# A fused cross-attention, attention and expert kernel: order of work at the two ends of its two-tile part, and fewer zero products at two norms

## What is computed

```python
# x: (1, 64, 256), context: (1, 6272, 256)
h = layernorm(x)
q = rmsnorm_per_head(h @ Wq.T); kv = context @ [Wk; Wv].T
k = rmsnorm_per_head(k_raw)                       # over the 8 numbers of each head
attn = softmax(q k^T * 8 ** -0.5)                 # 32 heads, 64 x 6272
x = x + attn @ v
x = x + self_attention(layernorm(x))              # 16 heads of 128, weights as codes times scales
x = x + experts(layernorm(x))                     # shared expert and 8 experts, top 2
```

## Time and profile before

| | us |
|---|---|
| median of 3 runs | 207.59 (207.58 to 207.79) |
| the profiled execution's own time | 208.22 |
| its span, first to last instruction | 206.4 |
| TensorE busy | 193.7 (94%) |
| ScalarE busy | 148.6 (72%) |
| VectorE busy | 124.7 (60%) |
| GpSimd busy | 109.5 (53%) |

### The profile page before, as it was taken

One profiled execution on the slowest core, in us unless ns is written; L12 is line 12 of the kernel. 1 busy time (PEld: TensorE's weight loads), 2 busy tenths in 40 slices (PEclk: granted clock), 3 DMA queues, 4 the chain that ended last, 5 costly groups with the idle time before them and its releaser, 6 DMA issues.

```text
span 206.4 us, 7072 instructions
## 1 busy us (share of the span) xinstructions
PE 193.7 (94%) x2625; PEld 133.0 (64%) x2625; DVE 124.7 (60%) x326; ACT 148.6 (72%) x286; POOL 109.5 (53%) x131
## 2 busy tenths in 40 slices
PE   7796987999999999999999999999997989999995
PEld 3364564777777777777777777777764553559554
DVE  1588868566767766677676667767533052463680
ACT  2474885889888888998888889888869912342240
POOL 6445759488666848857684885768475001000100
PEclk9999999999999999999999999999999999999999
DMA  6679999999999999999899899999985599100000
GB/s 195 174 195 205 169 234 213 211 175 245 248 208 237 215 223 233 173 259 210 216 210 240 215 210 254 207 259 203 254 198 110 174 405 430 64 0 3 3 0 13
DMA packets 66549, 39.70 MB, mean 192 GB/s; under 512 B 53858, under 2 KB 60642, under 8 KB 66402
## 3 DMA queue, kind: packets, MB, share of 16 engines
q1 hardware_dynamic: 66098, 38.98, 85.8%
q10 hardware_dynamic: 432, 0.46, 0.7%
HBM read 26.52 MB, written 0.07 MB: 129 GB/s over the span
## 4 chain that ended last, share of the span: by engine, by line
PE 71%; ACT 7%; issue 6%; DMA 5%; DVE 5%; POOL 3%; SPq 1%; DVEq 0%; ACTq 0%; POOLq 0%
PE ps L885 17%; PE ps L907 10%; PE ps L862 10%; PE ps L910 8%; PE ps L913 8%; PE ps L960 5%; ACT room L464 4%; DMA kT<-k 3%; PE ps L1054 3%; DMA wkv_f<-xwkv 2%; PE ps L1013 2%; PE ps L1072 2%; PE ps L819 1%; POOL w_all L385 1%; PE ps L999 1%
## 5 line engine op out<-in xcount | busy, mean ns | idle before, releaser
L464 ACT ACTIVATE room<-ps 128x1024 f32<-128x1024 f32 x98 | 95.3, 1023 | 1.8 <-PE ps L862 1.6
L403 POOL TENSOR_TENSOR ctx_lo<-ctx_f,ctx_hi 128x256 fp32r<-128x256 f32 x49 | 36.0, 734 | 43.6 <-DVE ctx_hi L640 40.6
L885 PE MATMUL ps<-room,v_sb 128*27 128x192 f32 (+1 forms) x1176 | 48.4, 310 | 0.2 <-ACT room L464 0.2
L907 PE MATMUL ps<-wkv_hi,ctx_hi 128*128 128x512 f32 x98 | 41.9, 428 | 2.4 <-DVE k L671 2.1
L910 PE MATMUL ps<-wkv_lo,ctx_hi 128*128 128x512 f32 x98 | 39.0, 398 | 1.2 <-DVE wkv_lo L592 1.2
L885 PEld LDWEIGHTS ps<-room,v_sb 128*27 128x27 f32 (+1 forms) x1176 | 32.8, 103 | 11.0 <-ACT room L464 0.6
L385 POOL TENSOR_TENSOR w_all<-w_all,s_ring 128x1024 f32<-128x1024 f32 x16 | 38.2, 2390 | 0.0
L647 DVE TENSOR_REDUCE k_ss<-k_sq 128x32 f32<-128x256 f32 x49 | 20.3, 415 | 29.2 <-ACT k_sq L471 29.2
L390 POOL TENSOR_TENSOR k<-k_n,k 128x256 f16<-128x256 f32 x49 | 32.9, 673 | 6.7 <-DVE k L671 6.7
L862 PE MATMUL ps<-q_blk,kT 48*128 48x128 f16 x784 | 31.5, 218 | 3.9 <-ACT room L464 2.1
L862 PEld LDWEIGHTS ps<-q_blk,kT 48*128 48x128 f16 x784 | 22.0, 94 | 19.1 <-issue 11.0
(11 more groups left out here) (117 smaller groups left out, 134.2 us busy)
## 6 DMA issues: line engine op xcount, KB each, us to landing
w_all<-codes SPq DMA_DIRECT2D x16, 512.0 KB, 4.2
ctx_f<-ctx_t SPq DMA_DIRECT2D x48, 128.0 KB, 3.6
up_sb<-up_w SPq DMA_DIRECT2D x5, 704.0 KB, 7.4
s_ring<-scales SPq DMA_DIRECT2D x12, 256.0 KB
s_ring<-wo_scales SPq DMA_DIRECT2D x4, 512.0 KB
dn_sb<-down_w SPq DMA_DIRECT2D x1, 1792.0 KB, 14.0
kT<-k SPq DMA_TRANSPOSE x49, 4.3
wkv_f<-xwkv SPq DMA_DIRECT2D x1, 256.0 KB, 3.9
```

Source lines behind the costliest of these rows:

```text
L403: nc.gpsimd.tensor_tensor(ctx_lo[:, split.slot(2)], ctx_f[:, split.slot(4)], ctx_hi[:, split.slot(2)].bitcast(F32), ALU.subtract).then_inc ...
L464: nc.scalar.activation(probs[:, t.probs_slot(), half], ps_scores[half].rearrange("p b n -> p (b n)"), ACT.Exp).then_inc(exp_done, 1)
L885: last = nc.tensor.matmul(ps_o[bank][CT * j:CT * j + heads * VW, at:at + heads * N], v_sb[:, t.slot(8), slot:slot + heads].rearrange("p h ...
L907: nc.tensor.matmul(dst, ctx_hi[:, a, c], wkv_hi[:, c], start=(c == 0), stop=False)
```

## The change

- `LOOP0` goes from 4 to 6: two more tiles ahead of the loop are written out, two fewer behind it. The number of trips stays 4.
- `singly` is true behind t = 44 in place of t = 42.
- TensorE, start: at t = 3 scores 3, values 2, projection 8; at t = 4 scores 4, projection 9, values 3.
- TensorE, end: at t = 43 scores 43, projection 48; at t = 44 scores 44, values 42 and 43.
- ScalarE, start: square 7, (3,0), root 7, (3,1), square 8, root 8; then (4,0), (4,1), square 9, root 9.
- ScalarE, end: (43,0), (43,1), square 48; then (44,0), root 48, (44,1).
- `keep_busy` 7 to 5 ahead of the norm of x1, 4 to 2 ahead of that of x2.

VectorE, GpSimd and SyncE keep their order.

```diff
-LOOP0 = 4
+LOOP0 = 6
@@ singly
-    return t.i is None and (t.c < PAIR0 or t.c > PAIR1)
+    return t.i is None and (t.c < PAIR0 or t.c > PAIR1 + 2)
@@ ScalarE, step
-                if not t.odd():
+                if t.i is None and t.c == PAIR0:
+                    keys_squared(r.ahead(-1))
+                    exps(t, 0)
+                    keys_rms(r.ahead(-1))
+                    exps(t, 1)
                     keys_squared(r)
-                if t.i is None and t.c == PAIR0:
+                    keys_rms(r)
+                elif t.i is None and t.c == PAIR1 + 2:
                     exps(t, 0)
-                    keys_squared(r.ahead(-1))
+                    keys_rms(r.ahead(-1))
                     exps(t, 1)
-                    keys_rms(r.ahead(-1))
                 else:
+                    squared_first = not t.odd() and not (t.i is None and t.c == PAIR0 + 1)
+                    if squared_first:
+                        keys_squared(r)
                     exps(t, 0)
                     exps(t, 1)
-                if t.odd():
-                    keys_squared(r)
-                keys_rms(r)
+                    if not squared_first:
+                        keys_squared(r)
+                    if t.i is not None or t.c <= PAIR1:
+                        keys_rms(r)
@@ TensorE, step
+            def all_values(pv):
+
+                for group in range(len(GROUPS)):
+                    if pv.exists():
+                        values(pv, group)
+
                 if singly(t):
-                    for group in range(len(GROUPS)):
-                        if pv.exists():
-                            values(pv, group)
+                    all_values(pv)
...
+                elif t.i is None and t.c == PAIR0:
+                    all_values(pv)
+                    project_context(kv)
+                elif t.i is None and t.c == PAIR0 + 1:
+                    project_context(kv)
+                    all_values(pv)
                 elif t.odd():
                     project_context(kv)
-                    project_context(kv.ahead(1))
+                    if kv.ahead(1).exists():
+                        project_context(kv.ahead(1))
                 else:
-                    for k in (pv.ahead(-1), pv):
-                        for group in range(len(GROUPS)):
-                            values(k, group)
+                    all_values(pv.ahead(-1))
+                    all_values(pv)
@@ TensorE, behind the tiles
-            keep_busy(7)
+            keep_busy(5)
...
-            keep_busy(4)
+            keep_busy(2)
```

## The result

| | before | after |
|---|---|---|
| median of 4 runs, us | 207.69 (207.58 to 208.18) | 204.40 (204.14 to 204.57) |
| the profiled execution's own time, us | 208.22 | 204.50 |
| its span, us | 206.4 | 202.5 |

The ratio is 0.9834 (95% interval 0.9817 to 0.9852). The change is worth 3.29 us between the medians; 3.14 had been forecast. In the changed kernel lines stand 5 to 8 further down: scores are L870, values L893, a projection L915, L918 and L921, zero products L827, the turning L818 and L821, keys times scales L679.

What follows compares the result with a forecast made beforehand. TensorE was taken to bound the two-tile loop and ScalarE its end, with a serial part behind. Start 1.02, end 1.72 and norms 0.40 sum to 3.14 us, taking the median from 207.59 to 204.45, range 203.9 to 205.6.

Steps and rivals of the forecast that it cites:

- The bound and the method: Whole kernel: TensorE bounds the loop, ScalarE the end, then a serial part; only the two ends and serial part change.
- Start, TensorE and ScalarE: Start of two-tile part: waits of 0.55 and 1.51 us go, projection 11 waits about 0.9 us, TensorE gains 1.15.
- Transposed keys, the cover of this: SyncE's queue at the start: keys of tile 4 keep 0.7 us of cover, about 1.3 us more slip stays hidden.
- the prediction's signs: Expected in the trace: projection 9 without wait, projection 11 near 37.9 after about 0.9 us for scaled keys, loop shifted 1.0.
- the list of what would be wrong: Keys 4 waiting over 1.3 us, transposed-key waits over 0.3 us from 130 to 145, or gaps between exponentials of tiles 45-48.
- the term of 1.02: Start's gain kept in the loop's steady state: 1.02 us, bounds 0.6 and 1.3.
- the leads of 0.88 and 1.15: Start of two-tile part: ScalarE's exponentials 5 come 0.88 us earlier, TensorE's projection 11 gains 1.15 us.
- rival A: Start gives little that lasts because transfers fix when keys land; 0.6 to 1.02 us lost, 205.05 to 205.47; chance 0.15.
- The loop: Late keys in the loop shift along with TensorE's pace: taken as 0, bounds 1.02 us loss and 0.3 gain.
- End: End of two-tile part: ScalarE's 1.79 us idle before square 48 goes, 1.72 us gained, bounds 1.0 and 1.8.
- Rival B: End gives half: late transposed keys of tiles 44-48 or scores 45 idle ScalarE 0.9 us; 205.35 us; chance 0.09.
- Norms: Two norms behind the tiles: fewer zero products gain 0.2 and 0.18 us, together 0.40, bounds 0.2 and 0.45.

Runs made afterwards that it cites:

- scales_late: Changed kernel with the 256 KB load of scales 2 issued behind keys 5 instead of ahead: 204.88 us, ratio 0.984 to the kernel before.
- keys6_held: Changed kernel with the transposition of keys 6 held on SyncE until keys 5 have landed: 206.88 us, ratio 0.9918 to the kernel before.
- loop_only: Kernel before with LOOP0 = 6 alone, same order of work on every engine: 207.92 us against 207.94, ratio 0.9987.
- norms_only: Kernel before with 5 and 2 zero products in place of 7 and 4 at the norms, nothing else: ratio 0.9943.
- end_tensor: Kernel before with TensorE's new order at the end alone, ScalarE's order there kept: 207.69 us, ratio 0.9984.
- end_only: Kernel before with the end's new order on TensorE and ScalarE alone, LOOP0 left at 4: ratio 0.9909.
- loop0_5: Changed kernel with LOOP0 = 5, the loop begun one tile earlier: 204.04 us, ratio 0.9824 to the kernel before.
- again: The changed kernel run once more, unaltered: 205.06 us, ratio 0.9875 to the kernel before.
- start_only: Kernel before with the start's new order on TensorE and ScalarE and LOOP0 = 6, end and norms as they were: ratio 0.9942.
- values2_behind: Changed kernel with scales 2 loaded behind keys 5 and projection 8 ahead of values 2 again: 204.03 us, ratio 0.9814 to the kernel before.

## Why the prediction held, step by step

**The bound and the method** held. The two ends and the two norms were the places to gain, and the pace of the loop did not change.

**Start, TensorE and ScalarE: right as far as it went.** Taken from 0.90 us earlier, as scores 3 were, the forecast times are values 2 28.3 (was 28.29), projection 8 29.3 (29.30), scores 4 30.9 (30.90), projection 9 31.45 (31.45), values 3 33.05 (33.04). Projection 9 without a wait, projection 11 waiting 0.50 us 9.07 behind scores 3 in `scales_late`: the order of events was the one worked out from ScalarE's steps.

**The step that failed is "Transposed keys, the cover of this".** It looked at the keys of tile 4 alone. Those were as said: landed 4.1 us after their issue, ahead of scores 4. The next tile was not looked at. Scores 5 stood at 36.96 in the kernel before, keys 5 were issued there at 29.94 and landed 4.5 us later, at about 34.5. The forecast moved scores 5 to 34.95 and so left 0.5 us of cover, where one transfer in the earlier trace rows needed 6.97: the risk could be read before. The issue did not shift (28.95, with the 0.90 of the head 29.85), the transfer took 6.6 us with the scales ahead of it, and the 1.51 us wait followed. So two of the prediction's signs were off: projection 11 stood at 37.67 + 0.90 = 38.57 in place of 37.9, without the wait for scaled keys, and the list of what would be wrong watches keys 4 alone.

**What that wait cost.** In the forecast a new wait of about 0.9 us for scaled keys stands ahead of projection 11. A wait for keys 5 takes its place up to that size, and only what exceeds it is lost. Over six executions the wait for keys 5 and the gain from scores 3 to scores 8 were 1.51/0.44, 1.39/0.58, 0.99/0.96, 0.88/1.07, 0.78/1.18 and none/1.18: gain = 1.18 less what the wait exceeds 0.8, to within 0.03 us. (`keys6_held` is left out, as its edit adds a wait of its own.) So the term of 1.02 was right in size when the keys come in time, 0.16 too low even, and this execution got 0.44. (The prediction does not work out how 1.02 follows from the leads of 0.88 and 1.15; it is their mean.) That is rival A's effect, at the low end of the price that it named (0.58 lost of 0.6 to 1.02), and its mechanism for one transfer: keys 5 were issued where they had been, while the step that wants them came 2 us earlier.

**The loop** was taken at 0 with up to 0.3 of gain if the delay of the late keys vanishes. It did vanish in this execution, and 0.31 us came of it, but that is chance and no part of the change. In the kernel before, scores 40 and 41 wait 0.20 and 0.07 us for late keys:

```profile
142.43 0.62 PE L862 MATMUL ps<-q_blk,kT 48*128 48x128 f16 x16 [0.20 <-DMA kT<-k]
```

From scores 8 to scores 43 ten of the fourteen traces take 104.08 us, in the old order (`loop_only`, `norms_only`, `end_tensor`) as in the new. The kernel before took 104.47, the changed kernel 104.16, `end_only`, which waits for such keys again, 104.56, and `loop0_5` 104.27.

**End: right**, 1.78 against 1.72, by the steps described: square 48 at 151.57 straight behind exponentials 43, root behind (44,0), nine exponentials in 8.61. This execution is a good one: over the nine traces with the new end the gain is 1.5 to 1.8 us. What the forecast did not say is how much each engine's order is worth; ScalarE's is two thirds of it. Rival B showed itself in small: in seven of the nine, scores 45 wait 0.11 to 0.32 us for their keys.

**Norms: right**, 0.43 against 0.40.

**The sum** hit by luck, in part. The start's missing 0.58 was mostly made up by 0.31 in the loop, which is chance, and by 0.06 at the end and 0.03 at the norms. That leaves 2.96 us where 3.14 were forecast; the 0.90 of the head is no part of the change. The medians lie 3.29 apart. A start that gives up to 1.18, as in `again`, would account for the difference, but the unprofiled executions have no trace that shows it.

## What to carry to other kernels

When a step is moved earlier on the bounding engine, check the cover of every transfer that feeds the steps behind it, not only of the first: here tile 4's keys had cover and tile 5's had not. When two waits stand in a row on one engine, removing the first can be free or worthless depending on what releases the second; price the last one. Filler products ahead of a wait could be cut here to about the length of that wait, but not to nothing.

## What the runs showed of the hardware beyond that

**The granted clock fell in seven of the fourteen traces, each time behind an idle of TensorE of 1 to 2 us.** It goes with a part of the spread of timed runs. Of the 33 executions of the kernel before in the first set, the 17 with a full mean clock took 207.10 to 208.28 us, the 13 with a mean of 0.991 or 0.992 took 207.59 to 209.81. It isn't all of it: the six executions of `start_only` with a full clock still lie from 206.11 to 208.11. In the profile of `start_only` the old end leaves TensorE idle for 1.06 us up to 154.11; then, in the table by stretches:

```profile
154.00:156.00 2.00, 1.80 (x40) 1.12 (x40) 1.02 (x2) 1.97 (x5) 0.35 (x1) 1.00 0.70 131
156.00:158.00 2.00, 1.60 (x24) 1.02 (x28) 0.00 (x0) 2.00 (x3) 2.00 (x2) 0.62 0.23 45
158.00:160.00 2.00, 2.00 (x40) 1.17 (x34) 0.00 (x0) 0.78 (x2) 0.64 (x1) 0.52 0.47 86
```

The clock is 0.62 and 0.52 there, the lower level of 1.2 GHz for most of both stretches, and values that take 1.07 us elsewhere took 1.93. The same idle of 1.06 us in the kernel before went without a fall, so a gap makes a fall possible, not certain. In `keys6_held` it fell behind the 1.95 us wait, in `again` from 18 us on, behind a wait of 1.31 us for the queries that ended at 16.53, and in the same place in `loop_only`, `scales_late` and `values2_behind` (the tables of the two kernels, by stretches):

```profile
38.00:40.00 2.00, 2.00 (x6) 1.62 (x5) 0.00 (x0) 1.38 (x2) 0.00 (x0) 0.50 0.90 173
```

```profile
18.00:20.00 2.00, 2.00 (x6) 1.45 (x6) 1.68 (x5) 1.14 (x3) 1.39 (x2) 0.50 1.02 178
```

A part of what the new end gives in the medians may be that it leaves no such gap. It is the smaller part: the nine executions of `end_only` with a full clock have a mean of 206.11 us, the 17 of the kernel before 207.64, and these 1.53 us lie within what the traces show.

**A transposition of one tile's keys by DMA took 3.0 to 7.2 us from issue to landing** over all traces, with a median of 4.3 in the kernel before and 4.7 in the changed one. Its issue on SyncE took 1.25 us or, behind the late one in the changed kernel, 3.35:

```profile
28.95 1.25 SPq L310 DMA_TRANSPOSE kT<-k  x1
...
30.92 3.35 SPq L310 DMA_TRANSPOSE kT<-k  x1
```
